# A graph network's edge weights: capping the exponentials in an instruction of their own, and multiplying the relation sums on GpSimd

## The reference, cut to what matters

```python
def _L1_gnn_ref(h, W, attn, rel_emb, src, dst, etype):
    rel_table = rel_emb.at[0].set(0.0)
    z = h @ W
    s_src = z @ attn[:d]
    s_dst = z @ attn[d:]
    e = jax.nn.leaky_relu(s_src[src] + s_dst[dst])
    m = jax.ops.segment_max(e, dst, num_segments=N)
    ex = jnp.exp(e - m[dst])
    denom = jax.ops.segment_sum(ex, dst, num_segments=N)
    alpha = ex / denom[dst]
    coef = rel_table[etype, 0] * alpha
    out = jax.ops.segment_sum(coef[:, None] * z[src], dst, num_segments=N)
```

## Time and profile before

| | |
|---|---|
| median of 3 runs | 3990.41 us (3985.39 to 3995.73) |
| the profiled execution | 3986.42 us, span 3984.6 us |
| granted TensorE clock, mean | 0.955 |
| busy: PE, DVE, ACT, POOL | 83%, 68%, 45%, 32% |
| stretch of the block with the change | 3222 to 3505 us of the span |

### The profile page before, as it was taken

The page is one execution under the profiler, slowest core; times in us unless marked ns, Lnnn a source line. Parts: engine busy times, 40 slices in busy tenths (PEclk is TensorE's granted clock), DMA queues, the critical chain, the costliest instruction groups (busy, mean ns, idle before and its releaser), DMA issues. The chain is left out here.

```text
span 3984.6 us, 91957 instructions
## 1 busy us (share of the span) xinstructions
PE 3301.9 (83%) x20966; PEld 2295.4 (58%) x20967; DVE 2690.4 (68%) x7939; ACT 1798.6 (45%) x4884; POOL 1291.7 (32%) x1218
## 2 busy tenths in 40 slices
PE   2429999999999878888888888888887967779499
PEld 2216666666666567777777777777743132234245
DVE  8715565656565489999999999999924669930601
ACT  1004444444444367767767777777713523320201
POOL 0017766666666633333333333333300000000100
PEclk9999999999999999999999999999967979979697
DMA  9982222222222256666666666666606968849195
GB/s 385 372 338 75 71 74 70 74 70 73 71 73 70 66 171 199 202 199 202 202 200 200 199 203 200 201 199 201 201 24 148 264 231 296 298 127 290 35 290 129
DMA packets 733537, 696.53 MB, mean 175 GB/s; under 512 B 51006, under 2 KB 680656, under 8 KB 726960
## 3 DMA queue, kind: packets, MB, share of 16 engines
q1 hardware_dynamic: 704466, 637.13, 52.8%
q0 software_dynamic: 25792, 54.52, 4.1%
q10 hardware_dynamic: 3230, 4.27, 0.3%
HBM read 340.81 MB, written 354.90 MB: 175 GB/s over the span
## 5 line engine op out<-in xcount | busy, mean ns | idle before, releaser
L843 POOL DMA_INDIRECT sorted_rows<-rows,posi x806 | 775.6, 962 | 441.6 <-issue 229.0
L950 POOL TENSOR_TENSOR hid<-pre_e,excess 128x512 f32<-128x512 f32 x376 | 481.9, 1282 | 1013.5 <-ACT excess L967 1013.5
L1099 DVE SCALAR_TENSOR_TENSOR acc<-acc,keep,pm 128x256 f32<-128x256 f32 x1504 | 717.1, 477 | 75.2 <-DVE acc L1099 35.7
L795 PE MATMUL s_peq<-sb_w1b,eT 64*128 64x128 f32 x1612 | 619.0, 494 | 87.2 <-DMA ef<-in_edge_attr_dram 62.3
L1026 PE MATMUL pm<-ohw_e,ohs_e 128*128 128x128 f32 x3008 | 662.4, 302 | 0.0
L795 PEld LDWEIGHTS s_peq<-sb_w1b,eT 64*128 64x128 f32 x1612 | 399.9, 309 | 294.6 <-issue 261.3
L1025 PE MATMUL pm<-ohd_e,ohs_e 128*128 128x128 bf16 x1504 | 334.3, 222 | 216.6 <-DVE acc L1099 201.7
L1032 PE MATMUL px<-PN,dT 128*128 x4512 | 498.3, 219 | 0.2 <-ACT dT L974 0.2
L982 ACT ACTIVATE ohw_e<-ohd_e,rt 128x128 f32<-128x128 bf16 x1504 | 474.6, 386 | 0.0
L1026 PEld LDWEIGHTS pm<-ohw_e,ohs_e 128*128 128x128 f32 x3008 | 459.5, 193 | 0.0
L967 ACT ACTIVATE excess<-pre_e 128x512 f32<-128x512 f32 x376 | 237.1, 631 | 436.5 <-DVE pre_e L1087 436.3
(11 more groups left out here) (283 smaller groups left out, 4735.6 us busy)
## 6 DMA issues: line engine op xcount, KB each, us to landing
count_matrices<-acc SPq DMA_DIRECT2D x1504, 128.0 KB, 1.9
ab<-count_matrices SPq DMA_DIRECT2D x75, 1600.0 KB, 14.8
sorted_rows<-zrow SPq DMA_DIRECT2D x188, 528.0 KB, 11.0
rt<-sorted_rows SPq DMA_DIRECT2D x376, 264.0 KB, 3.0
arb<-count_matrices SPq DMA_DIRECT2D x25, 1664.0 KB, 6.5
arb<-count_matrices SPq DMA_DIRECT2D x25, 1536.0 KB, 6.3
ef<-in_edge_attr_dram SPq DMA_DIRECT2D x60, 364.0 KB
sorted_rows<-rows,posi POOLq DMA_INDIRECT x806
```

The lines of the kernel that those rows point to most:

```text
L795: nc.tensor.matmul(pe_q[:, k % 2, 0:D], eT[:, k % 2, :], w1b[:], start=True, stop=True).then_inc(s_q, 1)
L843: pool.indirect_dma_start(sortd, bass.IndirectOffsetOnAxis(ap=posi[:, h, c:c + 1], axis=0), rows[:, h, c, :], None).then_inc(s_sc[h], 16)
L950: nc.gpsimd.tensor_tensor(hid[:, k % 2, :, 0:D], pre[:, k % 2, :, :], excess[:, k % 2, :, :], ALU.add).then_inc(s_g, 1)
L1099: nc.vector.scalar_tensor_tensor(acc[:, k % 2, j, :], before, keep[:, at:at + 1] if isinstance(at, int) else keep[:, ds(at, 1)], pm[:, j / ...
```

## The change

The cap at 2 becomes an instruction of its own on VectorE, a tensor and a constant, into a new buffer `ec`. VectorE then computes `tmp2` alone, and GpSimd computes `rx`, both from `ec`. Two semaphores come with it: `s_cl` (capped) and `s_pgo`, which GpSimd only counts up. `exponent` now waits for the capping instead of for `rx`, and the capping waits for `rx` and `tmp2` of the step before, which read the same half of `ec`. TensorE's, ScalarE's and SyncE's code is as before.

```diff
+                ec = ctx.enter_context(nc.sbuf_tensor("ec", [P, NT, P], F32))
...
+                s_cl = sem("w_clamped")
+                s_pgo = sem("w_pool_passed")
...
                         if not first:
-                            dve.wait_ge(s_rx, s * 2 + h - 1)
+                            dve.wait_ge(s_cl, s * 2 + h - 1)
                         nc.vector.scalar_tensor_tensor(ex[:, h, 0:b - a, :], RBv[:, 0, a:b, :], ss[:, 3, ds(s, 1)],
                                                        RBv[:, 1, a:b, :], ALU.add, ALU.max).then_inc(s_t, 1)
...
-                            e = ex[:, h, 0:b - a, :]
                             dve.wait_ge(s_e, s * 2 + h + 1)
+                            if not first:
+                                dve.wait_ge(s_rx, s * 2 + h - 1)
+                                dve.wait_ge(s_ax, s * 2 + h - 1)
+                            nc.vector.tensor_scalar(ec[:, a:b, :], ex[:, h, 0:b - a, :], 2.0, None, ALU.min).then_inc(s_cl, 1)
+                            dve.wait_ge(s_cl, s * 2 + h + 1)
                             dve.wait_ge(s_ld[h], s * 16 + 16)
                             if not first:
                                 dve.wait_ge(s_mm, s * 2 + h - 1)
 
-                            nc.vector.scalar_tensor_tensor(tmp2[:, a:b, :], e, 2.0, arb[:, a:b, 0, :], ALU.min,
-                                                           ALU.mult).then_inc(s_ax, 1)
-                            nc.vector.scalar_tensor_tensor(rx[:, a:b, :], e, 2.0, arb[:, a:b, 1, :], ALU.min,
-                                                           ALU.mult).then_inc(s_rx, 1)
+                            nc.vector.tensor_tensor(tmp2[:, a:b, :], ec[:, a:b, :], arb[:, a:b, 0, :], ALU.mult).then_inc(s_ax, 1)
...
+                @block.gpsimd
+                def _(pool):
+                    def step(s, first):
+                        for h, (a, b) in enumerate(HALF):
+                            pool.wait_ge(s_cl, s * 2 + h + 1)
+                            pool.wait_ge(s_ld[h], s * 16 + 16)
+                            if not first:
+                                pool.wait_ge(s_mm, s * 2 + h - 1)
+                            pool.sem_inc(s_pgo, 1)
+                            nc.gpsimd.tensor_tensor(rx[:, a:b, :], ec[:, a:b, :], arb[:, a:b, 1, :], ALU.mult).then_inc(s_rx, 1)
+                    step(0, True)
+                    with pool.Fori(1, NT) as s:
+                        step(s, False)
```

## The result

| | before | changed |
|---|---|---|
| median | 3990.42 us (3985.39 to 3995.73) | 4105.42 us (4101.79 to 4108.84) |
| ratio | | 1.0288 (95% interval 1.027 to 1.0306) |
| profiled execution | 3986.42 us, span 3984.6 | 4108.84 us, span 4107.1 |

A forecast was written before the change was run, and what follows sets the result against it. VectorE alone was taken to bound the block's 11.02 us step. VectorE's 9.39 plus GpSimd's 7.09 less handovers gave 15.94, +122 us in all: 4108.4 us profiled, 4112 as median, range 4075 to 4140.

The forecast's parts named there:

- VectorE alone set the step before: Edge-weights block: VectorE's six instructions fill the 11.02 us step with 11.03 us; every other engine waits for it.
- The terms: Block's instruction prices: cappings 0.96 and 1.03 us, `tmp2` as L1566 (1.75, 1.88), GpSimd's `rx` 3.41 and 3.68.
- They don't run at once: In the block, VectorE and GpSimd wait for each other's whole instructions, so 9.39 and 7.09 us a step add up.
- four places of the old trace: Outside the block, records stretched beside the other engine: 1.65 for 1.27, 2.04 for 1.54, 1.70 for 0.49 us, 784 for 684 ns.
- The overlaps that I listed: Handovers in each half: 0.14 us twice, 0.08 exponent to capping, against a 0.10 wait before `tmp2`; taken as -0.27.
- The order: In each half: capping, `tmp2`, then `rx` on GpSimd with the next exponent waiting under it; neither engine starves.
- The sum: Block's total: +4.92 us a step, +123 over 25 steps, -1 for the first capping, so +122 us.
- The rival on TensorE's clock: TensorE, half idle in the block, granted 1.2 GHz: at most 1 us a step, 4137 us; 9% together with other cases.
- the slack which I had counted: Block: from second-half `rx` to its next exponential takes 5.21 us, while the capping needing it comes some 9.5 us later.
- The first rival: Block: only the capping contends, exponents and `tmp2` run under `rx`; -0.95 us a step, -24, 3966 us; 4%.
- the second: Block: GpSimd waits but VectorE's two-tensor instructions pass it; step 12.2 us, +30, 4020 us; 7%.

The follow-up runs named there:

- e8: Kernel before with two buffers for the counts and relation sums, nothing else changed: ratio 0.9998, step 10.96 us.
- e1: Changed kernel with the relation product back on VectorE, capping still separate, GpSimd unused in the block: ratio 1.0083 to before, step 12.76 us.
- e3: Changed kernel without the capping, both products reading the exponentials straight: ratio 1.0175 to the kernel before, step 14.04 us.
- e2: Changed kernel with GpSimd multiplying only 6 of the 12 or 13 tiles of each half: ratio 1.0080 to before, step 12.41 us.
- e4: Changed kernel plus 14 short blocks pairing one VectorE with one GpSimd instruction kind; single execution; two-SBUF-tensor form with GpSimd's product: 2.07 us a round.
- e10: As e7, with the relation product moved to GpSimd, without a capping: ratio 0.9962 to the kernel before, step 10.25 us.
- r1_after: The changed kernel itself on another chip: 4105.8 us against 3982.3 for the kernel before, ratio 1.0318, step 15.92 us.
- e7: Kernel before with the exponent moved to ScalarE and two buffers for the counts and relation sums: ratio 0.9861, step 8.40 us.
- e9: As e7, with two buffers for the stationary matrix: 3907.1 us against 3982.3 for the kernel before, ratio 0.9801, step 7.77 us.

## Why the prediction was right, point by point

- *VectorE alone set the step before.* Shown by e8 (a freed load changes nothing) and by e1 (adding 1.97 us to VectorE lengthens the step by 1.74).
- *The terms.* Capping 0.96 and 1.03 forecast, 0.95 and 1.01 measured; `tmp2` 1.75 and 1.88, measured 1.76 and 1.89; GpSimd's product carried from 512 and 640 columns to 3.41 and 3.68, measured 3.43 and 3.70 once the wait for `tmp2` is taken off. One product of 1664 columns in e3 ran undisturbed, from 3869.86, and took 3.69. The straight line through two short sizes held up to 2.6 times the length.
- *They don't run at once.* The forecast read this from four places of the old trace; e2, e4 and e10 show it directly. The step was forecast at 15.94 and is 15.92. Part of that closeness is luck in small terms. The overlaps that I listed add up to 0.26 a half, not 0.27, so 0.52 a step where 0.54 was taken off; measured, 0.59 goes (9.38 and 7.13 against 15.92). From VectorE to GpSimd it is the 0.14 that I took, from GpSimd to VectorE 0.20. Capping to `tmp2` is 0.21 in the first half and 0.04 in the second, 0.12 where I took 0.10. GpSimd's products are 0.04 us a step longer than forecast, and the deviations nearly cancel.
- *The order* was as forecast: `tmp2` goes 0.13 us ahead of GpSimd, the exponent waits under `rx`, and in e4 the two take turns and neither starves.
- *The sum* was +122 on the profiled execution, which shows +122.4. The medians differ by 115 in the first measurement and by 123.5 in r1_after; the runs of one kernel scatter by 7 to 10 us there, so the 7 between forecast and median say nothing.
- *The rival on TensorE's clock* was argued away with the wrong reason. I wrote that idle time in every step had not lowered it before. But TensorE then idled 0.78 us ahead of these products; now it idles 2.54, and 0.50 is granted from 3402.94 to 3408.85 (0.81 in the block, 0.96 before), so that the products of a half take 5.91 us instead of 3.06. The price was nothing nonetheless. The exponential that waits for them ends at 3410.95, and the capping that needs it starts at 3412.31, when VectorE has got through the exponent: 1.36 us to spare. The steps are 15.89 to 15.93 us long. That the slack which I had counted (5.21 us against 9.5) was wide enough to swallow this too is luck; I had priced the case at up to 1 us a step.
- *The first rival*, VectorE relieved by the offload, is out by e3 and e4; *the second*, VectorE passing GpSimd, by the exponent's 5.0 and 5.39 us.

## What to carry to other kernels

Before work is given to GpSimd to relieve VectorE, look at what VectorE runs at that time: against a product on GpSimd, an instruction with two SBUF tensors, or with a tensor and a constant from SBUF to SBUF, has its time added, not hidden. One with a tensor from PSUM, or with a tensor and a constant into PSUM, ran undisturbed. Since GpSimd also takes twice as long for a column (2.09 against 1.035 ns), such a move could only lose in this block, where all of VectorE's instructions were of the first kinds; ScalarE, which has no part in this, could take work here (e7, e9). In a profile look for records that are longer than the same shape elsewhere: a held-up instruction counts as busy, and the busy share does not tell its wait from work.

## What the runs showed of the hardware that I had not expected

Whichever starts first goes first, by however little, and then the two take strict turns. VectorE's `tmp2` starts 0.13 us ahead in the changed kernel, and GpSimd waits; GpSimd's product starts 0.01 and 0.02 us ahead in e4's first two pairs, and VectorE waits. From there one instruction of each follows the other, 2.07 us a round, although VectorE's block holds eight without a wait between them and GpSimd's four. I had expected the turns in e4, but not said which side begins. And the transfers of the counts reached 416 GB/s in e9, where the 290 GB/s of the kernel before at a busy share of 0.79 had made me expect some 360.
